# Attention scores as keys x queries, turned by VectorE blocks and a DRAM exchange, with the attention's engine programs in a new order

## The reference

```python
def reference(x, ctx_4096, pos_BxS2, mask_BxSxS2_ik0, g_xattn, g_ffn, Wq, Wk, Wv, Wo, w12, b12, w3, b3):
    # x, ctx: (8, 128, 512); 32 query heads, 8 key/value heads, D = 128
    def attn(query, key, value, position_ids, src_mask):
        q = (query @ Wq).reshape(8, 128, 32, 128).transpose(0, 2, 1, 3)
        k = (key @ Wk).reshape(8, 128, 8, 128).transpose(0, 2, 1, 3)
        v = (value @ Wv).reshape(8, 128, 8, 128).transpose(0, 2, 1, 3)
        q = q * cos + rotate_half(q) * sin
        k = k * cos + rotate_half(k) * sin
        k, v = jnp.repeat(k, 4, axis=1), jnp.repeat(v, 4, axis=1)
        scores = jnp.einsum('bhqd,bhkd->bhqk', q, k) / sqrt(128)
        scores = jnp.where(src_mask[:, None] == 0, -1e9, scores)
        p = jax.nn.softmax(scores, axis=-1)
        o = jnp.einsum('bhqk,bhkd->bhqd', p, v)
        return o.transpose(0, 2, 1, 3).reshape(8, 128, 4096) @ Wo
    x = x + tanh(g_xattn) * attn(layernorm(x), ctx, ctx, pos, mask)
    x12 = layernorm(x) @ w12.T + b12
    x1, x2 = split(x12, 2)
    return x + tanh(g_ffn) * ((silu(x1) * x2) @ w3.T + b3)
```

## Time and profile before

| | us |
|---|---|
| median of 3 runs | 644.98 |
| lowest, highest | 642.45, 645.43 |
| the profiled execution | 644.58 |
| its span, first to last instruction | 642.8 |

### The profile page before, as it was taken

The page is one execution under the profiler, slowest core; times in us unless marked ns, Lnnn a source line. Parts: engine busy times, 40 slices in busy tenths (PEclk is TensorE's granted clock), DMA queues, the critical chain, the costliest instruction groups (busy, mean ns, idle before and its releaser), DMA issues.

```text
span 642.8 us, 10433 instructions
## 1 busy us (share of the span) xinstructions
PE 632.7 (98%) x3105; PEld 526.7 (82%) x3105; DVE 512.7 (80%) x1235; ACT 316.5 (49%) x891; POOL 450.8 (70%) x374
## 2 busy tenths in 40 slices
PE   8999999998999999999999999999999999999997
PEld 7888888786888888788888778888888888888886
DVE  3987665898988898889888888889887998985342
ACT  4435622545555555554555446555554557555210
POOL 6457866998888987898898788888887667502000
PEclk9999999999999999999999999999999999999999
DMA  9997995254454444436444354535434404100002
GB/s 301 318 332 212 305 301 163 90 173 139 164 156 133 152 144 147 132 132 192 138 144 147 119 162 149 164 116 174 137 114 134 131 0 114 37 2 0 1 33 98
DMA packets 101735, 93.23 MB, mean 145 GB/s; under 512 B 8240, under 2 KB 78384, under 8 KB 101680
## 3 DMA queue, kind: packets, MB, share of 16 engines
q1 hardware_dynamic: 100256, 91.52, 45.0%
q0 software_dynamic: 384, 1.05, 0.5%
q10 hardware_dynamic: 1040, 0.00, 0.1%
HBM read 60.30 MB, written 32.24 MB: 144 GB/s over the span
## 4 chain that ended last, share of the span: by engine, by line
PE 96%; DVE 1%; issue 1%; DMA 1%; ACT 0%; SPq 0%; DVEq 0%
PE f_bank L603 13%; PE f_bank L605 12%; PE f_bank L604 12%; PE o_bank L603 10%; PE o_bank L605 10%; PE o_bank L604 10%; PE s_banks L726 6%; PE pv_bank L603 3%; PE pv_bank L605 3%; PE pv_bank L604 3%; PE s_banks L727 2%; PE t_bank L603 1%; PE t_bank L605 1%; PE s_banks L605 1%; PE s_banks L604 1%; PE t_bank L604 1%
## 5 line engine op out<-in xcount | busy, mean ns | idle before, releaser
L1015 ACT ACTIVATE prob<-prob,small 128x128 f32<-128x128 f32 x256 | 99.7, 391 | 40.3 <-DVE small L1559 40.0
L603 PE MATMUL f_bank<-xT_hi,wq_hi 128*128 128x512 f32 x256 | 103.1, 403 | 0.3 <-DVE t_sin L1467 0.3
L603 PE MATMUL o_bank<-wo_hi,o_hi 128*128 128x512 f32 x248 | 98.4, 397 | 2.9 <-issue 2.4
L605 PE MATMUL f_bank<-xT_hi,wq_lo 128*128 128x512 f32 x256 | 100.1, 391 | 0.0
L604 PE MATMUL f_bank<-xT_lo,wq_hi 128*128 128x512 f32 x256 | 100.1, 391 | 0.0
L605 PE MATMUL o_bank<-wo_hi,o_lo 128*128 128x512 f32 x248 | 97.2, 392 | 0.0
L604 PE MATMUL o_bank<-wo_lo,o_hi 128*128 128x512 f32 x248 | 96.8, 390 | 0.0
L945 ACT ACTIVATE pT_hi<-p 128x512 fp32r<-128x512 f32 x51 | 32.3, 634 | 126.6 <-DMA p<-p_scratch 126.6
L1283 POOL TENSOR_TENSOR q<-t_cos,t_sin 128x512 f32<-128x512 f32 x64 | 82.9, 1295 | 16.5 <-DVE t_sin L1467 16.3
L1467 DVE TENSOR_TENSOR t_sin<-f_bank,rope 64x512 f32<-64x512 f32 x128 | 88.1, 688 | 2.7
L1292 POOL TENSOR_TENSOR prob<-prob,small 128x512 f32<-128x512 f32 x64 | 66.6, 1041 | 29.1 <-DVE small L1569 28.7
(11 more groups left out here) (173 smaller groups left out, 1472.1 us busy)
## 6 DMA issues: line engine op xcount, KB each, us to landing
p_scratch<-p_blk SPq DMA_DIRECT2D x51, 256.0 KB, 2.1
p<-p_scratch SPq DMA_DIRECT2D x51, 256.0 KB, 3.1
k_scratch<-ks_parts SPq DMA_DIRECT2D x16, 512.0 KB, 3.1
raw<-in_L_xattn_Wq_dram SPq DMA_DIRECT2D x32, 256.0 KB, 2.9
raw<-in_L_xattn_Wo_dram SPq DMA_DIRECT2D x32, 256.0 KB, 2.7
k_parts<-k_scratch SPq DMA_DIRECT2D x16, 512.0 KB, 4.8
v_scratch<-vs_hi SPq DMA_DIRECT2D x16, 256.0 KB, 3.9
v_scratch<-vs_lo SPq DMA_DIRECT2D x16, 256.0 KB, 4.1
```

Of the source, the lines that this page charges most:

```text
L603: nc.tensor.matmul(dst, st[0], mv_[0], start=start, stop=False)
L605: return nc.tensor.matmul(dst, st[1], mv_[0], start=False, stop=stop)
L1015: e = nc.scalar.activation(prob[:, k, h, :], prob[:, k, h, :], ACT.Exp, bias=nmin[k][:, h:h + 1], scale=-1.0, accum_out=psum_row[k][:, h:h ...
```

## The change

Units 4 to 51 (ST0 to ST1) have their scores made the other way round, keys on the partitions: `three` matmuls of 512 columns each, with the two parts of the keys as the stationary operand. They are brought to queries x keys as the probabilities are turned, by a transpose of blocks on DVE (`score_blocks`) into `s_blk`, a store to DRAM and a load with blocks exchanged into `s32`. The exchange permutes positions inside a batch, so POOL writes the rotated queries and keys of these units in a permuted order (`apart` and `together`, a step of 32 elements on the output), and the mask is copied once into that order (`mfill2`, by ACT). The mask and the row minimum then come in one pass of four reducing instructions per unit that read `s32` and `mfill2`, both in SBUF (`mask_turned`); `mask_first` is gone for these units. `p_blocks` reads their probabilities with 32 elements on end where it read every fourth. Each of the two score banks in PSUM holds one unit now. The programs of all engines for the attention are written as lines, one call each, in a new order; which of head and tail units are turned by PE stays.

```diff
+ST0, ST1 = 4, 52
+    s_dram = nc.dram_tensor("s_scratch", [4 * 128, GH * S], F32, kind="Internal").ap()
+        s_blk = place("s_blk", [128, 2, GH * S], F32, at["cT_lo"])
+        s32 = place("s32", [128, 2, GH * S], F32, at["cT_lo"] + 4096)
+        mfill2 = place("mfill2", [128, B, S], F32, at["cT_lo"] + 8192)
+        def turned(n):
+            return ST0 <= n < ST1
+        def apart(t):
+            return t.rearrange("p (b j a) -> p b a j", b=HB, j=4)
+        def together(t):
+            return t.rearrange("p (b a j) -> p b a j", b=HB, j=4)
...
+            def store_s(n):
+                k, slot = n % 2, n % 4
+                sp.wait_ge(dve_sblk, n + 1 - ST0)
+                sp.dma_start(s_dram[slot * 128:(slot + 1) * 128, :], s_blk[:, k, :]).then_inc(s_stored[k], 16)
+            def load_s(n):
+                k, slot, m = n % 2, n % 4, (n - ST0) // 2
+                sp.wait_ge(s_stored[k], 16 * (m + 1))
+                if m:
+                    sp.wait_ge(dve_mask, n - 1)
+                sp.dma_start(s32[:, k, :].rearrange("p (j x) -> p j x", j=4),
+                             s_dram[slot * 128:(slot + 1) * 128, :].rearrange("(j b) (i x) -> (b i) j x", j=4, i=4)).then_inc(s_loaded[k], 16)
...
+                if turned(n):
+                    if n < ST0 + 2:
+                        pe.wait_ge(dve_mask, ST0)
+                    else:
+                        pe.wait_ge(dve_sblk, n - 1 - ST0)
+                    three(s_banks[:, 512 * k:512 * k + 512], (k_parts[:, half, b, 0:S], k_parts[:, half, b, S:2 * S]),
+                          (q_hi[:, k].rearrange("p h s -> p (h s)"), q_lo[:, k].rearrange("p h s -> p (h s)")), True, True).then_inc(pe_score, 1)
+                    return
...
-                nc.gpsimd.tensor_tensor(q32[:, (e // 4) % 2, e % 4, :], t_cos[:, ts, :], t_sin[:, ts, :], ALU.add).then_inc(pool_rope, 1)
+                dst, c, s = q32[:, (e // 4) % 2, e % 4, :], t_cos[:, ts, :], t_sin[:, ts, :]
+                if turned(16 * gg + 4 * (e // 4)):
+                    dst, c, s = apart(dst), together(c), together(s)
+                nc.gpsimd.tensor_tensor(dst, c, s, ALU.add).then_inc(pool_rope, 1)
...
+            def score_blocks(gg, c, k):
+                n = n_of(gg, c, k)
+                dve.wait_ge(pe_score, n + 1)
+                if n >= ST0 + 2:
+                    dve.wait_ge(s_stored[k], 16 * ((n - ST0) // 2))
+                nc.vector.transpose(s_blk[:, k, :].rearrange("p (i h a) -> p i h a", i=4, h=GH),
+                                    s_banks[:, 512 * k:512 * k + 512].rearrange("p (h i b) -> p i h b", h=GH, i=4)).then_inc(dve_sblk, 1)
+            def mask_turned(gg, c, k):
+                n = n_of(gg, c, k)
+                dve.wait_ge(s_loaded[k], 16 * ((n - ST0) // 2 + 1))
+                prob_free(n)
+                if n == ST0:
+                    dve.wait_ge(act_mask2, 1)
+                scores = s32[:, k, :].rearrange("p (j h a) -> p h j a", j=4, h=GH)
+                fill = mfill2[:, n % B, :].rearrange("p (j a) -> p j a", j=4)
+                for h in range(GH):
+                    op = nc.vector.tensor_tensor_reduce(prob[:, k, h, :].rearrange("p (j a) -> p j a", j=4), scores[:, h], fill, 1.0, HUGE,
+                                                        ALU.add, ALU.min, nmin[k][:, h:h + 1])
+                op.then_inc(dve_mask, 1)
...
+                keys = prob[:, k].rearrange("p h (j a) -> p j h a" if turned(n) else "p h (a j) -> p j h a", j=4)
                 nc.vector.transpose(p_blk[:, k, :].rearrange("p (j h b) -> p j h b", j=4, h=GH),
-                                    prob[:, k].rearrange("p h (a j) -> p j h a", j=4)).then_inc(dve_pblk, 1)
+                                    keys).then_inc(dve_pblk, 1)
...
-            def step(gg, c, k):
-                mask_scores(gg, *unit(c, k, 1))
-                o_lo_split(gg, *unit(c, k, -2))
-                cos_q(gg, 6 + 2 * c + k)
-                recip(gg, *unit(c, k, 1))
-                sin_q(6 + 2 * c + k)
-                p_blocks(gg, *unit(c, k, 1))
-                add_out(gg, *unit(c, k, -2))
...
+            recip(*u(28))
+            sin_q(34)
+            p_blocks(*u(28))
+            score_blocks(*u(30))
+            mask_turned(*u(29))
+            o_lo_split(*u(26))
+            add_out(*u(25))
+            cos_q(0, 35)
+            recip(*u(29))
```

More of the change, by code:

```diff
@@ L1353, in _ @@
+            split_chunk(*pair_chunks(*u(3)[:2])[1])
+            norm(*u(4))
             add_q(0, 9)
[L1354 to L1362 removed]
+            q_lo_split(*u(7))
+            norm(*u(5))
+            add_q(0, 10)
@@ new lines, in _ @@
+            add_out(*u(2))
+            recip(*u(6))
+            p_blocks(*u(6))
+            cos_q(0, 12)
+            score_blocks(*u(8))
+            o_lo_split(*u(4))
+            mask_turned(*u(7))
+            sin_q(12)
+            recip(*u(7))
+            o_lo_split(*u(5))
+            add_out(*u(3))
+            p_blocks(*u(7))
+            cos_q(0, 13)
+            score_blocks(*u(9))
+            sin_q(13)
+            mask_turned(*u(8))
+            cos_q(0, 14)
+            sin_q(14)
@@ new lines, in _ @@
+            recip(*u(8))
+            score_blocks(*u(10))
+            add_out(*u(4))
+            p_blocks(*u(8))
+            mask_turned(*u(9))
+            o_lo_split(*u(6))
+            recip(*u(9))
+            cos_q(0, 15)
+            sin_q(15)
+            p_blocks(*u(9))
+            o_lo_split(*u(7))
+            score_blocks(*u(11))
+            add_out(*u(5))
+            mask_turned(*u(10))
+            cos_q(0, 16)
+            recip(*u(10))
+            add_out(*u(6))
+            sin_q(16)
@@ new lines, in _ @@
+            mask_turned(*u(13))
+            o_lo_split(*u(10))
+            cos_q(0, 19)
+            recip(*u(13))
+            add_out(*u(9))
+            sin_q(19)
+            p_blocks(*u(13))
+            score_blocks(*u(15))
+            o_lo_split(*u(11))
+            mask_turned(*u(14))
+            cos_q(0, 20)
+            add_out(*u(10))
+            recip(*u(14))
+            sin_q(20)
+            p_blocks(*u(14))
+            score_blocks(*u(16))
+            mask_turned(*u(15))
@@ new lines, in _ @@
+            o_lo_split(*u(12))
+            recip(*u(15))
+            cos_q(0, 21)
+            sin_q(21)
+            p_blocks(*u(15))
+            add_out(*u(11))
+            add_out(*u(12))
+            score_blocks(*u(17))
+            o_lo_split(*u(13))
+            mask_turned(*u(16))
+            cos_q(0, 22)
+            recip(*u(16))
+            sin_q(22)
+            p_blocks(*u(16))
+            score_blocks(*u(18))
+            mask_turned(*u(17))
+            o_lo_split(*u(14))
@@ new lines, in _ @@
+            o_lo_split(*u(23))
+            add_out(*u(22))
+            recip(*u(26))
+            cos_q(0, 32)
+            sin_q(32)
+            p_blocks(*u(26))
+            score_blocks(*u(28))
+            mask_turned(*u(27))
+            o_lo_split(*u(24))
+            add_out(*u(23))
+            cos_q(0, 33)
+            recip(*u(27))
+            sin_q(33)
+            p_blocks(*u(27))
+            score_blocks(*u(29))
+            o_lo_split(*u(25))
+            mask_turned(*u(28))
```

1790 lines of the change are left out of this document (1492 added, 298 removed).

## The result

The changed kernel takes 743.41 us (median of four runs, 741.98 to 747.14), the kernel before 644.68 beside it: a ratio of 1.155, with a 95% interval of 1.150 to 1.160. It is slower, as forecast, and inside the range, but 29 us over the predicted 714. The profiled execution has a span of 741.2 us.

The account below looks back on a forecast made before the run. TensorE bounded the kernel before; VectorE would be late after. VectorE's 6.1 us plus 2.26 of waits and 0.22 for exponentials gives 8.6 us per unit against 7.17, +69 us over 48 units: forecast 714 us, range 636 to 790.

Parts of the forecast that it names:

- TensorE, -9.2 us: Attention, units 4 to 51: three wide score matmuls take 0.68 us instead of 0.87, saving 9.2 us in all.
- the lock: At mask_turned, VectorE with two SBUF inputs and GpSimd run one at a time, each for a whole instruction.
- VectorE's own work: VectorE per unit: mask_first goes, score_blocks comes, p_blocks shortens; 6.33 us becomes 5.94, or 6.1 with short idle times.
- the bound of 1.11 for score_blocks: score_blocks: upper transpose time of 1.11 us against the 0.70 taken; VectorE would then need 6.5 us per unit.
- The exclusion: mask_turned's two-SBUF-input reductions take turns with GpSimd's instructions: first wait 0.5 us, a further one 1.16 us.
- How many waits: Four reductions of a unit: mean 2.5 waits for GpSimd, 2.26 us per unit; two to four in the range.
- The walk: VectorE and GpSimd stepped by their durations through four units from recip(28), counting waits at the reductions: mean 2.5.
- (8.6 - 7.17) x 48: Attention stage: VectorE's forecast 8.6 us per unit against 7.17 before, over 48 units: +69 us.
- The rest: GpSimd's strided writes (at most +18 us), DMA, exchange and mask_columns taken at nothing; new order of head and tail +-3 us.
- 1 (VectorE keeps the interface over its four reductions): mask_turned: only the first reduction waits for GpSimd; 634 to 648 us, 641 taken; chance 0.16.
- 2 (a custom instruction takes no part): mask_turned: custom reductions are not subject to the exclusion and TensorE stays the bound; 635 us; chance 0.14.
- 3 (exchange late; its 7.8 us should read 7.9): Score store and load grow from 5.2 to 7.8 us, mask_turned waits 0.5 us per unit; 660 us; chance 0.07.

## Why the prediction was right, and where 29 us were missing

**TensorE, -9.2 us.** The kernel with the mask in PSUM has this term and not the lock: -6.9 us. Its scores take 332.66 - 331.98 = 0.68 us on TensorE, as in the sum (timeline, to hold against the earlier trace rows):

```profile
331.98 0.39 PE L889 MATMUL s_banks<-q_hi,k_parts 128*128 128x512 f32 x1
...
332.66 0.39 PE L889 MATMUL f_bank<-xT_hi,wq_hi 128*128 128x512 f32 x1
```

So TensorE's work shrank as forecast, and 2.3 us of the gain did not come out. TensorE stood idle 5.35 us in the stage instead of 2.88, and the new order of head and tail is in the 6.9 too; which of them took the 2.3 us is open.

**VectorE's own work, 5.94 us busy per unit.** Both block transposes came out as taken, 716 and 710 ns against 0.70; the bound of 1.11 for score_blocks was not needed. With the mask in PSUM, where nothing waits for GpSimd, VectorE is busy 270.53 / 330 x 6.89 = 5.65 us per unit (6.89 from its reciprocals). 0.3 less than the sum.

**The exclusion.** Right, and shown from three sides: taken away, put into the kernel before, and halved. A further wait was priced at 1.16 us and measured 1.06 to 1.09 (1.34 to 1.37 less 0.28).

**How many waits.** The walk had three, two, two and three waits in units 29 to 32. The trace has (durations of the four reductions in us) 0.94, 1.35, 1.34, 0.28; 0.60, 1.37, 0.28, 0.28; 0.93, 1.34, 0.28, 0.28; 0.65, 1.37, 1.37, 0.28: three, two, two, three. Those four units wait 2.12 us in the mean, all 48 wait 100.6 / 48 = 2.10, and 2.26 were forecast.

**The step that failed: (8.6 - 7.17) x 48.** It sets VectorE's work, its waits and 0.40 us of idle time (0.18 of short gaps, 0.22 for exponentials in one unit of four) against the period of before, as if VectorE, once late, ran with hardly a gap. The trace has (330 - 280.95) / 330 x 9.21 = 1.37 us idle per unit: about 1 us more, and with the 0.3 us less of own work and somewhat under 0.1 us less of waiting (280.95 / 330 x 9.21 - 5.65 = 2.19 in the stage) that is the 0.6 us between 8.6 and 9.21, times 48 the missing 29 us. The idle time alone would have missed by 47 us; the too large own work hid 14 of them, which is luck. The table shows what would have been nearer: with a delay at the reductions, the idle time that VectorE has in a kernel that TensorE bounds does not close. 644.6 - 6.9 + 100.6 = 738 us from the measured terms; from the terms on record, 644.6 - 9.2 + 48 x 2.26 = 744.

The sum had no term for TensorE's lower clock either. By the estimate above at most 0.36 of the 1.37 us came from it by way of the scores, 17 of the 29 us. The rest does not need it: the kernel before with two SBUF inputs stood idle (330 - 295.09) / 330 x 9.12 = 0.96 us per unit at a granted clock of 0.98 (9.12 from its reciprocals), and its delay cost its full length.

Why the gaps stay is seen in two places of the changed kernel. VectorE's reductions of unit 24 (timeline) end late, o_lo stands behind them:

```profile
331.95 0.65 DVE L2511 CUSTOM_DVE_ANT_0 prob<-s,mfill 128x128 f32<-128x128 f32 x1 [0.54 <-DMA s<-s_scratch]
...
335.30 0.68 DVE L2367 TENSOR_TENSOR o_lo<-pv_bank,o_hi 128x512 fp32r<-128x512 f32 x1
...
339.06 0.72 DVE L2498 STREAM_TRANSPOSE s_blk<-s_banks 128x512 f32<-128x512 f32 x1 [0.87 <-PE s_banks L891]
```

TensorE (timeline) waits for that o_lo, and the scores stand behind the waiting matmul in its queue:

```profile
331.95 0.39 PE L890 MATMUL f_bank<-xT_lo,wq_hi 128*128 128x512 f32 x1
332.18 0.39 PE L891 MATMUL f_bank<-xT_hi,wq_lo 128*128 128x512 f32 x1
336.13 0.76 PE L889 MATMUL pv_bank<-pT_hi,v_hi 128*128 128x512 f32 x1 [3.56 <-DVE o_lo L2367]
...
337.54 0.63 PE L889 MATMUL s_banks<-q_hi,k_parts 128*128 128x512 f32 x1
337.97 0.63 PE L890 MATMUL s_banks<-q_lo,k_parts 128*128 128x512 f32 x1
338.39 0.63 PE L891 MATMUL s_banks<-q_hi,k_parts 128*128 128x512 f32 x1
```

The scores come when VectorE has already got to score_blocks, which waits 0.87 us for them. The queue is not alone here: six matmuls at 0.23 instead of 0.43 us would have ended some 1.2 us earlier, an estimate. The other place has the granted clock at 1.00. There a reduction has just waited 1.36 - 0.28 = 1.08 us (timelines of VectorE, then TensorE, and TensorE's window):

```profile
276.78 1.36 DVE L2511 CUSTOM_DVE_ANT_0 prob<-s,mfill 128x128 f32<-128x128 f32 x1
...
278.50 0.68 DVE L2367 TENSOR_TENSOR o_lo<-pv_bank,o_hi 128x512 fp32r<-128x512 f32 x1
...
283.73 0.72 DVE L2498 STREAM_TRANSPOSE s_blk<-s_banks 128x512 f32<-128x512 f32 x1 [1.05 <-PE s_banks L891]
```

```profile
279.33 0.47 PE L889 MATMUL pv_bank<-pT_hi,v_hi 128*128 128x512 f32 x1 [1.56 <-DVE o_lo L2367]
...
283.31 0.39 PE L891 MATMUL s_banks<-q_hi,k_parts 128*128 128x512 f32 x1
```

```profile
279.30:283.80 4.50, 4.47 (x20) 3.71 (x21) 3.38 (x7) 3.01 (x10) 2.82 (x3) 1.00 0.22 69
```

TensorE waits 1.56 us for the late o_lo, works without a pause up to the scores, and score_blocks waits 1.05 us for them: VectorE's own delay comes back to it through another engine's queue. The moved reciprocal suggests the same of ScalarE and GpSimd. That this holds for every gap was not shown.

**The rest.** add_q with its strided writes takes 1308 ns (1295 before): taken at nothing, rightly. The exchange is hidden: mask_turned waited 0.6 us for it in the whole stage. GpSimd was to lose 0.2 us per turn; its subtractions last 1.31 us instead of 1.30, so its part is nearly free.

**The rivals.** 1 (VectorE keeps the interface over its four reductions) falls: in unit 29 the second and the third wait too. 2 (a custom instruction takes no part) falls; its 635 us is what the kernel with the mask in PSUM gives, 636.9, where there is nothing to take part in. 3 (exchange late; its 7.8 us should read 7.9) falls with the 0.6 us; with the mask in PSUM, at the DMA share of 0.70 that it names, mask_turned waited 5.3 us for it in the stage, 0.1 per unit instead of 0.5.

## What to carry to other kernels

Before an operand of a VectorE instruction moves from PSUM to SBUF, count its SBUF inputs: with two of them it waited here, by turns, for one GpSimd instruction each time, and a second operand kept in a spare PSUM bank took all of that away (106 us for one ScalarE copy every fourth unit). And when a late engine is fed through other engines' in-order queues, do not count its idle share in a kernel that another engine bounds as slack: here only some 0.2 us per unit of it was, for a delay at the head of the softmax.

## What the runs showed of the hardware that was not expected

- A GpSimd subtraction of 128x256 takes 0.76 us and one of 128x512 1.31: by these two, an estimate of 0.2 us per instruction does not depend on the columns. Cutting its instructions in two halved each wait (1.06 to 0.54 us) but took only 18% off their sum (100.6 to 82.8).
- GpSimd writes with a step of 32 elements at 1.308 us against 1.295, while VectorE's block transpose reads with a step of four at 1.107 against 0.71.
- TensorE was busy 80 to 81% of the stage in the changed kernel and in the kernel before with two SBUF inputs, but its granted clock was 0.92 in the one and 0.98 in the other. TensorE's waits differ in length: the changed kernel has eight of over 3 us in the stage, the longest 7.6; the other has two, of 3.2 and 5.2, and all the rest there are of 1.4 to 1.73 us. That the length decides was not shown.
